# A softmax product skewed by two steps, and two engines given work ahead of the expert stages

## The chip, the cores and the metric

The kernel runs on one core of a Trainium2 chip. The core has five engines that run their own instruction streams and meet at semaphores: TensorE (matmuls, from weights that a separate instruction loads), VectorE, ScalarE (activation functions, from a table that has to be loaded for each family of functions), GpSimd (POOL) and SyncE (SP), which mostly issues DMAs. Matmuls write to PSUM, eight banks of 128 partitions by 512 float32. The metric is the device time of one execution in microseconds; lower is better.

## The reference

Six residual layers on x of shape (4, 1024, 128), each on a layer norm of x: a top-4-of-32 expert layer, a linear attention, the expert layer again, a top-2-of-8 expert layer with exact gelu ("L1_ffn"), a softmax attention ("L1_attn"), and the top-2 layer again. The change touches the last three and the two gates ahead of them. Cut to what matters:

```python
def _L1_attn_ref(x, P_q, P_k, P_v, P_o):           # x (4, 1024, 128), 16 heads of 64
    logits = einsum('bhmk,bhnk->bhmn', Q, K) * sqrt(64)
    logits = where(causal, logits, -inf)
    key_weights = softmax(logits, axis=-1)
    o = einsum('bhmm,bhmv->bhmv', key_weights, V)   # the diagonal of the weights only
    return einsum('bhmv,hdv->bmd', o, P_o)

def _L1_ffn_ref(x, Wg, W1, b1, W2, b2):             # 8 experts, 512 hidden, top 2
    gates = softmax(xt @ Wg)                        # idx1, idx2, w1, w2 from them
    xe[idx1, pos1] += xt; xe[idx2, pos2] += xt      # rows sorted by expert
    h = gelu(einsum('ecd,edf->ecf', xe, W1) + b1)
    ye = einsum('ecf,efd->ecd', h, W2) + b2
    return ye[idx1, pos1] * w1 + ye[idx2, pos2] * w2
```

So softmax needs of every query only the diagonal weight: exp(own score - max) over the sum of exp(score - max).

## The kernel before

**Order of stages.** `program()` builds eleven stages and each engine runs its part of them one after another: setup, the gated expert layer, keys and queries of the linear attention, `sorted_ffn` (the second gated layer, whose tail also routes and sorts rows for the top-2 experts), `moe_experts`, `moe_combine`, `softmax_diagonal`, `sorted_ffn` once more (values and output of the softmax attention, with the routing of the last layer), `moe_experts`, `moe_combine`. The order of work on each engine is written out by hand; there is no scheduler.

**Softmax** (`softmax_diagonal`, L2678 on). A unit is one pair of heads of one batch: 8 pairs times 4 batches, 32 units. Both heads of a pair lie in the 128 partitions, head 0 in rows 0 to 63 and head 1 in rows 64 to 127, so each score matmul uses 64 rows of TensorE. `ORDER = (1, 5, 6, 4, 2, 3, 7)` is the order of the query blocks q of 128 queries; block q has (q + 1) x 128 keys. Blocks 4 to 7 are done by `big` (L2841): for each head two halves of (q + 1) x 64 columns (320, 384, 448 and 512), each in its own bank, and each as three passes over high and low parts of the operands, so 6 matmuls a head, 12 a product. Blocks 0 to 3 are done by `little` (L2863). Each unit also projects the keys and queries of the unit after next (`project`, L2820, four groups of three matmuls of 512 columns, L2829 to L2831) and sums the diagonal scores (`diagonals`, L2855).

For each block and head VectorE adds the causal mask and takes the minimum (`lowest`, L2968), and ScalarE then does exp with the sum of the row (`exps`, L2949, at L2950), both in the score banks. VectorE works head 0, then head 1 of a block, and so does ScalarE. The eight banks go round as a ring (`first_bank`), and `wait_bank` makes TensorE wait until the last user of a bank is done: mostly the exponential of an earlier block (`exp_done`), for the first banks after the projections ScalarE's or VectorE's copy of a projection (`out_act`, `out_dve`). For example block 4 gets the banks of block 5, head by head, and block 7 those of block 4.

In `big` of before all four banks, of both heads, are waited for first, and then head 0 and head 1 take turns matmul by matmul:

```python
for a in range(2):
    for k in range(2):
        wait_bank(pe, (first_bank(u, n) + 2 * a + k) % BANKS, "exp_done", scored_before(u, n, a) + 1)
for p, (qs, ks) in enumerate(passes(u)):
    for k in range(2):
        for a in range(2):
            last = pe.matmul(...)
```

**Expert stages** (`moe_experts`). 23 blocks of 512 sorted rows. SP loads the rows of a block from HBM (`rows_from`) once all of them have been sent there: it waits for `sent`, the semaphores of the indirect DMAs that GpSimd issues in `send_rows` (L812 on). TensorE turns them (`turn`, L2274), ScalarE and VectorE make the high and low parts (L2354, L2406), TensorE makes four up-products of three matmuls (L2286 to L2288), ScalarE does gelu (L2332) and the rounded copy (L2340), VectorE the low part (L2378) and copies the expert's weights to where TensorE reads them (L2385, L2394), TensorE makes the down-products (L2298 to L2300). `iterations` starts with an iteration c = -1 that only turns block 0. TensorE enters after `sorted`, which VectorE sets at the end of `positions`. ScalarE's last work before is the exp of the gates (L1499).

## Time and profile before

| | us |
|---|---|
| runs | 1681.05, 1692.07, 1695.04 (median 1692.07) |
| profiled execution | 1686.52, span 1684.5 |
| TensorE matmul busy | 1409.7 (84%), 7981 instructions |
| VectorE busy | 1342.9 (80%) |
| ScalarE busy | 1034.0 (61%) |
| GpSimd busy | 859.0 (51%) |
| mean granted TensorE clock | 0.946 of full speed |

The first expert stage's head lies at about 654 us, its blocks run to about 815; softmax runs from about 874 to 1333; the second expert stage's head lies at about 1481 us. In the rows a line such as L2850 is a line of the kernel before, PE is TensorE's matmuls and PEld its weight loads, DVE is VectorE, ACT ScalarE. A row's last bracket is the idle time of the engine before it and what ended it. A group with x12 is twelve instructions in a row, and its duration runs from the first start to the last end. The granted clock is 1.00 at 2.4 GHz and 0.50 at 1.2 GHz.

### The profile page before, as it was taken

What the parts mean: (1) busy time and instruction counts of PE and PEld (TensorE: products, weight loads), DVE (VectorE), ACT (ScalarE), POOL (GpSimd) and SP (SyncE); (2) the same over time, 40 slices, a digit from 0 to 9 for tenths busy, and PEclk for the clock granted to TensorE, in tenths of its full rate; (3) what the DMA queues carried; (4) which work ended last, traced back from release to release, by engine and by line L of the source; (5) the groups of instructions that cost most, each with busy time, mean ns of one, the idle gap of its engine ahead of it and who ended that gap; (6) DMA issues with size and microseconds to landing.
All of it is one profiled execution on the core that took longest, in us unless ns stands there. A gap on an engine that the chain in (4) does not pass through costs nothing.

```text
span 1684.5 us, 29060 instructions
## 1 busy us (share of the span) xinstructions
PE 1409.7 (84%) x7981; PEld 1029.5 (61%) x7981; DVE 1342.9 (80%) x3812; ACT 1034.0 (61%) x2178; POOL 859.0 (51%) x743
## 2 busy tenths in 40 slices
PE   5999999898999994999358888888888799679990
PEld 4777877655656663777236665566566566457770
DVE  7699999567676766787679999999999777858876
ACT  7544442374232326888469999999989623268880
POOL 5856753210133342666656666666666225627662
PEclk9999999999999996999779999999999899879995
DMA  9990010000011104232299700000000001123225
GB/s 197 182 180 15 1 26 26 2 1 13 20 32 43 32 21 100 61 79 67 73 195 182 119 1 1 1 1 1 1 1 2 1 14 38 42 56 73 67 60 150
DMA packets 182167, 91.61 MB, mean 54 GB/s; under 512 B 43829, under 2 KB 176902, under 8 KB 182048
## 3 DMA queue, kind: packets, MB, share of 16 engines
q1 hardware_dynamic: 167840, 71.19, 23.2%
q0 software_dynamic: 9984, 16.89, 3.1%
q10 hardware_dynamic: 4224, 2.10, 0.4%
q8 instruction: 56, 0.92, 0.2%
q14 instruction: 63, 0.52, 0.1%
HBM read 32.59 MB, written 61.18 MB: 56 GB/s over the span
## 4 chain that ended last, share of the span: by engine, by line
PE 56%; DVE 16%; ACT 11%; issue 7%; DMA 3%; POOL 3%; DVEq 2%; SPq 1%; POOLq 0%; ACTq 0%
PE psum L1371 9%; PE psum L2850 8%; ACT psum L2950 7%; PE psum L660 5%; PE psum L661 4%; PE psum L662 4%; DVE psum L2970 4%; PE psum L2829 2%; PE psum L2830 2%; PE psum L2831 2%; DVEq L2418 2%; PE psum L1126 1%; DMA answers<-ed,answer_to 1%; PE psum L1128 1%; PE psum L1127 1%
## 5 line engine op out<-in xcount | busy, mean ns | idle before, releaser
L2970 DVE CUSTOM_DVE_ANT_0 psum<-psum,cmask 128x128 f32<-128x128 f32 (+7 forms) x512 | 375.1, 786 | 23.8 <-PE psum L2850 23.5
L2950 ACT ACTIVATE psum<-psum,gate 128x128 f32<-128x128 f32 (+7 forms) x512 | 367.0, 719 | 41.7 <-DVE gate L2970 34.4
L2462 POOL DMA_INDIRECT answers<-ed,answer_to x184 | 199.4, 1084 | 82.5 <-issue 47.4
L1371 PE MATMUL psum<-raw_all,w 128*128 128x512 f32 x384 | 196.6, 595 | 1.5 <-DVE raw_all L1512 1.5
L660 PE MATMUL psum<-xl,wreg 128*128 128x512 f32 x320 | 181.9, 568 | 2.6 <-ACT psum L2950 1.3
L1510 DVE SCALAR_TENSOR_TENSOR raw_all<-psum,hg 128x512 f32<-128x512 f32 x128 | 88.1, 690 | 58.5 <-PE psum L662 56.9
L2850 PE MATMUL psum<-spare_sets_room 64*128 64x384 f32 (+3 forms) x768 | 91.9, 371 | 43.1 <-ACT psum L2950 43.1
L2850 PE MATMUL psum<-hh,hl 64*128 64x384 f32 (+3 forms) x768 | 91.9, 371 | 41.9 <-ACT psum L2950 41.9
L661 PE MATMUL psum<-xh,wreg 128*128 128x512 f32 x320 | 126.9, 397 | 0.0
L662 PE MATMUL psum<-xh,wreg 128*128 128x512 f32 x320 | 126.7, 396 | 0.0
L2850 PEld LDWEIGHTS psum<-spare_sets_room 64*128 64x128 f32 x768 | 70.0, 190 | 67.4 <-ACT psum L2950 55.8
L2378 DVE TENSOR_TENSOR hl<-gate,hh 128x512 fp32r<-128x512 f32 x92 | 63.3, 688 | 59.7 <-ACT hh L2340 35.7
L2850 PEld LDWEIGHTS psum<-hh,hl 64*128 64x128 f32 x768 | 70.2, 191 | 66.4 <-ACT psum L2950 52.8
L1240 POOL TENSOR_TENSOR hl<-hg,hh 128x512 fp32r<-128x512 f32 x65 | 86.1, 1329 | 44.2 <-ACT hh L1172 37.3
L2950 ACT ACTIVATION_READ_ACCUMULATOR psum<-psum,gate 128x1 f32 x512 | 105.0, 205 | 0.0
L824 POOL DMA_INDIRECT rows<-raw_all,row_no x64 | 61.8, 965 | 74.5 <-PE psum L662 61.8
L824 POOL DMA_INDIRECT rows<-row,row_no x64 | 62.0, 969 | 64.8 <-PE psum L662 50.3
L1172 ACT ACTIVATE hh<-hg 128x512 fp32r<-128x512 f32 x86 | 54.1, 633 | 65.7 <-DVE hg L1203 63.8
L201 POOL TENSOR_TENSOR spare_p<-spare_p 128x1 f32<-128x1 f32 x63 | 18.3, 290 | 140.7 <-DVE row_no L785 66.6
L660 PEld LDWEIGHTS psum<-xl,wreg 128*128 128x128 f32 x320 | 61.3, 192 | 38.4 <-issue 26.5
L1371 PEld LDWEIGHTS psum<-raw_all,w 128*128 128x128 f32 x384 | 72.4, 189 | 20.2 <-DVE raw_all L1512 2.2
L661 PEld LDWEIGHTS psum<-xh,wreg 128*128 128x128 f32 x320 | 61.4, 192 | 32.6 <-issue 28.1
(437 smaller groups left out, 4051.3 us busy)
## 6 DMA issues: line engine op xcount, KB each, us to landing
rows<-blank SPq DMA_DIRECT2D x146, 258.0 KB, 7.2
row<-rows SPq DMA_DIRECT2D x46, 256.0 KB
raw_all<-answers SPq DMA_DIRECT2D x32, 256.0 KB, 4.2
w<-in_L_ffn_W_dram SPq DMA_DIRECT2D x16, 256.0 KB, 3.0
answers<-ed,answer_to POOLq DMA_INDIRECT x184
x<-in_L_attn_x_dram SPq DMA_DIRECT2D x4, 512.0 KB, 5.8
out_dram<-x ACTq DMA_DIRECT2D x8, 256.0 KB, 4.6
rawD<-in_L_ffn_values_dram SPq DMA_DIRECT2D x4, 256.0 KB, 6.9
```

The source lines that it names most:

```text
L660: pe.matmul(dst, wh, xl[:, blk(i)], start=start, stop=False)
L661: pe.matmul(dst, wl, xh[:, blk(i)], start=False, stop=False)
L662: return pe.matmul(dst, wh, xh[:, blk(i)], start=False, stop=stop)
L824: pool.indirect_dma_start(rows, bass.IndirectOffsetOnAxis(ap=row_no[:, i % 2, c, t:t + 1], axis=0), row_of(i)[:, t, c, :], None).then_inc( ...
L1240: pool.tensor_tensor(hl[:, j % SLOTS, :], kept[n % len(kept)], hh[:, j % SLOTS, :].bitcast(F32), ALU.subtract).then_inc(S["lo_pool"], 1)
L1371: pe.matmul(bank(B_OUT[i % 2]), col(dn, j), hidden[:, n % HID, :], start=(j == 0), stop=(j == nf - 1)).then_inc(S["dn_done"], 1)
L1510: last = dve.scalar_tensor_tensor(out, raw, 0.0, gates_now, ALU.max, ALU.mult)
L2378: dve.tensor_tensor(hl[:, j, :], hid[j], hh[:, j, :].bitcast(F32), ALU.subtract).then_inc(S["lo_done"], 1)
L2462: pool.indirect_dma_start(answers, bass.IndirectOffsetOnAxis(ap=answer_to[:, out.odd, t:t + 1], axis=0), y_row[:, out.odd, t, :], None, bo ...
L2850: last = pe.matmul(big_scores(u, n, a)[:, k, :], head(qs, a, q * P, P), head(ks, a, k * half, half), start=(p == 0), stop=(p == 2))
L2950: return act.activation(src, src, ACT.Exp, bias=kept_at(arg, u, q, a), scale=-1.0, accum_out=kept_at(esum, u, q, a))
L2970: return dve.tensor_tensor_reduce(src, src, mask, 1.0, 3e38, ALU.add, ALU.min, kept_at(arg, u, q, a))
```

## The change

Three edits. `big` issues head 0's six matmuls two steps ahead of head 1's (`SKEW = 2`): steps 0 and 1 of head 0 alone, then four steps of both in turn, then steps 4 and 5 of head 1 alone; and each bank is waited for just before its first matmul, not all four ahead. `keep_awake` runs matmuls of 512 bf16 columns whose result is not used, into bank 0: 7 at the entry of each expert stage, after waiting for `sent` of all rows, and 3 in the iteration c = -1, behind the turn of block 0. ScalarE runs one Gelu on a small tile (4 columns) after the exp of the gates, into `rs`, whose content is no longer needed; it waits for the last layer norm step first.

```diff
--- before.py
+++ after.py
@@ -824,6 +824,11 @@
                 pool.indirect_dma_start(rows, bass.IndirectOffsetOnAxis(ap=row_no[:, i % 2, c, t:t + 1], axis=0),
                                         row_of(i)[:, t, c, :], None).then_inc(S["sent"][i % 2], 16)
 
+    def keep_awake(pe, times):
+
+        for _ in range(times):
+            pe.matmul(bank(0), onesb[:], m16[:].rearrange("p e t -> p (e t)"), start=True, stop=True)
+
     def count_all(pe, S):
 
         pe.wait_ge(S["place_step"], PLACES * NB)
@@ -1497,6 +1502,8 @@
                 heads_turned(act, H)
             act.wait_ge(S["logits_scaled"], 1)
             act.activation(G, L, ACT.Exp).then_inc(S["exp_done"], 1)
+            act.wait_ge(S["step"], NORMS * NB)
+            act.activation(rs[:], mv[:, :, 1], ACT.Gelu)
 
         def vector(dve):
             def apply_gates(i, j):
@@ -2311,6 +2318,8 @@
                 for j in range(Q):
                     if j == 0 and (b + 1).there():
                         turn(b + 1)
+                    if j == 0 and not b.loop and b.c == -1:
+                        keep_awake(pe, 3)
                     if b.there():
                         up(b, j)
                     if (b + -1).there():
@@ -2319,6 +2328,9 @@
                         back(b + -2)
 
             pe.wait_ge(before["sorted"], 1)
+            for a in range(2):
+                pe.wait_ge(before["sent"][a], 16 * 2 * BT * (NB // 2))
+            keep_awake(pe, 7)
             iterations(pe, one)
 
         def scalar(act):
@@ -2699,6 +2711,7 @@
         ORDER = (1, 5, 6, 4, 2, 3, 7)
         LITTLE = {1: (1,), 2: (2, 0), 3: (3,)}
         DIAG, QUARTERS = 1, 4
+        SKEW = 2
         NS = 2 * len(ORDER)
         BANKS_OF = [4 if q >= BT else 2 for q in ORDER]
         PER_UNIT = NP + sum(BANKS_OF)
@@ -2841,16 +2854,23 @@
             def big(u, n):
                 q = ORDER[n]
                 half = wide(q) // 2
-                for a in range(2):
-                    for k in range(2):
+                steps = [(p, k) for p in range(3) for k in range(2)]
+
+                def step(a, m):
+                    p, k = steps[m]
+                    qs, ks = passes(u)[p]
+                    if p == 0:
                         wait_bank(pe, (first_bank(u, n) + 2 * a + k) % BANKS, "exp_done", scored_before(u, n, a) + 1)
-                for p, (qs, ks) in enumerate(passes(u)):
-                    for k in range(2):
-                        for a in range(2):
-                            last = pe.matmul(big_scores(u, n, a)[:, k, :], head(qs, a, q * P, P),
-                                             head(ks, a, k * half, half), start=(p == 0), stop=(p == 2))
-                            if p == 2 and k == 1:
-                                last.then_inc(S["scored"], 1)
+                    last = pe.matmul(big_scores(u, n, a)[:, k, :], head(qs, a, q * P, P),
+                                     head(ks, a, k * half, half), start=(p == 0), stop=(p == 2))
+                    if m == len(steps) - 1:
+                        last.then_inc(S["scored"], 1)
+
+                for m in range(len(steps) + SKEW):
+                    if m < len(steps):
+                        step(0, m)
+                    if m >= SKEW:
+                        step(1, m - SKEW)
 
             def diagonals(u):
                 g, b = which(u)
```

On TensorE, in softmax, from the diagonals (L2859, after: L2879) to the 320-column product, in a unit in the middle of a batch. The names in brackets are those of the first owner of a semaphore, which is used again here: `f0_oT_ready` is `exp_done`, `a0_kv_done` is `out_dve`, `a0_f_done` is `out_act`. Before:

```order
L2859 MATMUL psum<-ed,pair_ones 32x256 [waits f0_xT_done]
L2859 MATMUL psum<-ed,pair_ones 32x256 x3
L2850 MATMUL psum<-spare_sets_room 128x384 [waits a0_kv_done,f0_oT_ready]
L2850 MATMUL psum<-spare_sets_room 128x384 x11
L2850 MATMUL psum<-spare_sets_room 128x448 [waits f0_oT_ready,a0_f_done]
L2850 MATMUL psum<-spare_sets_room 128x448 x11
L2850 MATMUL psum<-spare_sets_room 128x320 [waits f0_oT_ready]
L2850 MATMUL psum<-spare_sets_room 128x320 x11
```

and of the change:

```order
L2879 MATMUL psum<-ed,pair_ones 32x256 [waits f0_xT_done]
L2879 MATMUL psum<-ed,pair_ones 32x256 x3
L2864 MATMUL psum<-spare_sets_room 128x384 [waits f0_oT_ready] x2
L2864 MATMUL psum<-spare_sets_room 128x384
L2864 MATMUL psum<-spare_sets_room 128x384 [waits a0_kv_done]
L2864 MATMUL psum<-spare_sets_room 128x384
L2864 MATMUL psum<-spare_sets_room 128x384 [waits a0_kv_done]
L2864 MATMUL psum<-spare_sets_room 128x384 x6
L2864 MATMUL psum<-spare_sets_room 128x448 [waits a0_f_done] x2
L2864 MATMUL psum<-spare_sets_room 128x448
L2864 MATMUL psum<-spare_sets_room 128x448 [waits f0_oT_ready]
L2864 MATMUL psum<-spare_sets_room 128x448
```

The row of the first matmul of a product carried all its waits; now four of its twelve matmuls carry one each: the first two of head 0, and the first of each half of head 1, with a matmul of head 0 between.

On TensorE, from the end of the gates (`count_all`, L831, after: L836) to the first up-product of the expert stage (L2286, after: L2293). Here `a0_f_ready`, `a0_scaled` stand for `x_load`, and `a0q_squared` for `xl_done`. Before:

```order
L831 MATMUL psum<-m,before 128x512 [waits f1_place_step,f1_g_copied,f1_hid_done]
L831 MATMUL psum<-m,onesb 128x512
L2274 MATMUL psum<-ident,row 128x128 [waits a0_f_ready,f1_sorted]
L2274 MATMUL psum<-ident,row 128x128 x3
L2274 MATMUL psum<-ident,row 128x128 [waits a0q_squared,a0_scaled]
L2274 MATMUL psum<-ident,row 128x128 x3
L2286 MATMUL psum<-xl,xh 128x512 [waits a0q_q_done,a0q_squared]
L2287 MATMUL psum<-xl,xh 128x512
```

and of the change:

```order
L836 MATMUL psum<-m,before 128x512 [waits f1_place_step,f1_g_copied,f1_hid_done]
L836 MATMUL psum<-m,onesb 128x512
L830 MATMUL psum<-m,onesb 128x512 [waits f1_sent1,f1_sent0,f1_sorted]
L830 MATMUL psum<-m,onesb 128x512 x6
L2281 MATMUL psum<-ident,row 128x128 [waits a0_f_ready]
L2281 MATMUL psum<-ident,row 128x128 x3
L830 MATMUL psum<-m,onesb 128x512 x3
L2281 MATMUL psum<-ident,row 128x128 [waits a0q_squared,a0_scaled]
L2281 MATMUL psum<-ident,row 128x128 x3
L2293 MATMUL psum<-xl,xh 128x512 [waits a0q_q_done,a0q_squared]
L2294 MATMUL psum<-xl,xh 128x512
```

Seven matmuls stand ahead of the first turn, with the waits for the row sends and for `sorted`, and three between the first and the second turn.

On ScalarE, from the exp of the gates (L1499, after: L1504) to the first gelu (L2332, after: L2344), before:

```order
L1499 ACT_TABLE_LOAD
L1499 ACTIVATE own<-own 128x256 [waits f1_logits_scaled]
L2354 ACTIVATE xl<-psum 128x512 [waits a0q_rooted,f1_sorted]
L2354 ACTIVATE xl<-psum 128x512 [waits a0q_rooted]
L2332 ACT_TABLE_LOAD [waits a0_ks_read]
L2332 ACTIVATE r<-psum,b_now 128x512 [waits a0q_den_done] x2
```

and of the change:

```order
L1504 ACT_TABLE_LOAD
L1504 ACTIVATE own<-own 128x256 [waits f1_logits_scaled]
L1506 ACT_TABLE_LOAD
L1506 ACTIVATE rs<-mv 128x4 [waits f1_step]
L2366 ACTIVATE xl<-psum 128x512 [waits a0q_rooted,f1_sorted]
L2366 ACTIVATE xl<-psum 128x512 [waits a0q_rooted]
L2344 ACTIVATE r<-psum,b_now 128x512 [waits a0_ks_read,a0q_den_done]
L2344 ACTIVATE r<-psum,b_now 128x512 [waits a0q_den_done]
```

The table load that stood behind the two rounded copies of rows, right ahead of the first gelu, now stands behind the exp. The instructions of VectorE, GpSimd and SP are the same in the same order.

## Rows read from the trace of the kernel before

**Rows 1.** Busy time by stretch: us, then busy (xinstructions) of each engine, granted clock, DMA

```profile
661.04:665.12 4.08, 4.08 (x12) 3.21 (x11) 1.44 (x4) 3.66 (x5) 0.00 (x0) 0.50 0.54 127
...
1488.21:1491.15 2.94, 2.94 (x9) 2.36 (x8) 1.44 (x4) 2.52 (x3) 0.00 (x0) 0.50 0.40 107
...
1021.49:1035.70 14.21, 11.59 (x95) 8.52 (x94) 13.45 (x36) 13.16 (x34) 9.14 (x6) 1.00 0.00 1
...
1166.88:1170.30 3.42, 3.42 (x28) 3.38 (x28) 2.50 (x7) 2.71 (x7) 3.42 (x2) 0.50 0.00 0
```

**Rows 2.** Timeline of one softmax unit: start us, us, engine, line, op [idle before, releaser]

```profile
1020.43 0.97 DVE L2970 CUSTOM_DVE_ANT_0 psum<-psum,cmask 128x768 f32<-128x768 f32 x1 [0.39 <-PE psum L2850]
...
1020.84 1.49 PE L2850 MATMUL psum<-hh,hl 64*128 64x448 f32 x12 [0.44 <-ACT psum L2950]
...
1021.31 1.00 DVE L2970 CUSTOM_DVE_ANT_0 psum<-psum,cmask 128x768 f32<-128x768 f32 x1
1021.49 0.88 ACT L2950 ACTIVATE psum<-psum,gate 128x768 f32<-128x768 f32 x1 [0.80 <-DVE gate L2970]
...
1022.33 1.10 DVE L2970 CUSTOM_DVE_ANT_0 psum<-psum,cmask 128x896 f32<-128x896 f32 x1
...
1023.65 1.14 PE L2850 MATMUL psum<-hh,hl 64*128 64x320 f32 x12 [1.33 <-ACT psum L2950]
...
1024.57 0.98 ACT L2950 ACTIVATE psum<-psum,gate 128x896 f32<-128x896 f32 x1
...
1024.80 0.83 DVE L2970 CUSTOM_DVE_ANT_0 psum<-psum,cmask 128x640 f32<-128x640 f32 x1 [0.27 <-PE psum L2850]
...
1025.73 0.77 ACT L2950 ACTIVATE psum<-psum,gate 128x640 f32<-128x640 f32 x1
...
1026.52 0.77 ACT L2950 ACTIVATE psum<-psum,gate 128x640 f32<-128x640 f32 x1
...
1027.65 1.65 PE L2850 MATMUL psum<-hh,hl 64*128 64x512 f32 x12 [0.86 <-ACT psum L2950]
...
1030.50 0.39 PE L2831 MATMUL psum<-xh,wreg 128*128 128x512 f32 x1
1030.50 0.19 PEld L2829 LDWEIGHTS psum<-xl,wreg 128*128 128x128 f32 x1
...
1030.72 0.39 PE L2829 MATMUL psum<-xl,wreg 128*128 128x512 f32 x1
...
1033.29 1.31 PE L2850 MATMUL psum<-spare_sets_room 64*128 64x384 f32 x12
...
1035.70 0.88 ACT L2950 ACTIVATE psum<-psum,gate 128x768 f32<-128x768 f32 x1 [0.81 <-DVE gate L2970]
```

**Rows 3.** Chain of waits in that unit: start us, us, what

```profile
1027.41 0.24 issue
```

**Rows 4.** Who waited for whom, 878 to 1320 us: total us, times, longest

```profile
DVE psum L2970 <- PE psum L2850: 21.9, 57, 1.2
```

**Rows 5.** Timeline of ScalarE, 1164 to 1180 us: q=5, head 0, of two units

```profile
1164.43 0.88 ACT L2950 ACTIVATE psum<-psum,gate 128x768 f32<-128x768 f32 x1 [0.81 <-DVE gate L2970]
...
1179.29 0.88 ACT L2950 ACTIVATE psum<-psum,gate 128x768 f32<-128x768 f32 x1 [0.83 <-DVE gate L2970]
```

**Rows 6.** Chain of waits of the whole span: the last row send

```profile
651.28 2.37 DMA rows<-row,row_no
```

**Rows 7.** Timeline of the first expert stage's head

```profile
657.65 1.09 PE L2274 MATMUL psum<-ident,row 128*128 128x128 f32 x4 [7.24 <-DMA row<-rows]
...
660.31 1.08 PE L2274 MATMUL psum<-ident,row 128*128 128x128 f32 x4 [1.56 <-DVE xl L2406]
...
662.04 1.28 ACT L2332 ACT_TABLE_LOAD   x1
...
663.34 1.34 ACT L2332 ACTIVATE r<-psum,b_now 128x512 f32<-128x512 f32 x2
...
666.89 0.40 PE L2298 MATMUL psum<-hh,xh 128*128 128x512 f32 x1
```

## The prediction

> **What bounds the kernel now.** I read the stretches by engine first, then who waited for whom in softmax, then one unit of softmax in order of time, last the head of an expert stage.
>
> Softmax is 32 units (8 pairs of heads, 4 batches), from about 878 to 1333 us. In a quiet unit no engine is full: VectorE 13.45, ScalarE 13.16, TensorE 11.59 of 14.21 us [rows 1]. What repeats is a loop through three engines, to be followed in [rows 2] (a "product" is a `big`, named by its columns per half; q is the row block). VectorE takes the minimum of q=5, head 0 (1020.43); ScalarE's exponentials of q=5, 6 and 4 follow almost without a gap (1021.49 to 1026.52 + 0.77, and the last is over, its sum read out, at 1027.41 [rows 3]); this frees the banks of the 512-column product (1027.65); behind it TensorE runs four projections, the small scores, the diagonals and the 384-column product (1033.29) without waiting; its head 0 starts VectorE 14.2 us after the first time. Exponentials start at 1021.49 and 1035.70: the period. VectorE waited for the products 21.9 us in 57 waits, 0.7 per unit [rows 4]. That 0.7 is the most that earlier scores can give back.
>
> The two expert stages start with a slow clock: granted 0.50, that is 1.2 of 2.4 GHz, while TensorE makes the first hidden products (661.04 to 665.12, and 1488.21 to 1491.15) [rows 1]. Before the first of them it had waited 7.24 us for the rows (657.65) [rows 7].
>
> **Softmax, part by part.** Nothing is added to the work: twelve matmuls as before, now in eight slots instead of six. A slot of 512 columns is 0.22 to 0.23 us (1030.50 to 1030.72) [rows 2]; scaled by columns, as an estimate, 0.17 for 384, 0.20 for 448, 0.14 for 320 (check: the twelve of 320 and of 512 columns take 1.14 and 1.65, 0.085 more a slot, the scale says 0.086).
> What the skew does to a product that waits: head 0 now asks only for its own banks, so its first steps run while head 1's exponential ends. After head 1's banks come free, head 0 needs three steps instead of six, head 1 still six. So head 0 is scored three slots earlier and TensorE is free at the same time as before. For one that doesn't wait, head 0 is as before and head 1 two slots later, the last of which the next product's head 0 can fill.
> - q=4, 320 columns (1023.65, waited 1.33): head 0 is there 0.42 earlier. VectorE had waited 0.27 (1024.80) and gets 0.27. ScalarE does not: its exponential before ends at 1024.57 + 0.98 = 1025.55 and the next could start at 1025.62 at the usual gap of up to 0.07, against 1025.73. Worth 0.11 to the loop.
> - q=6, 448 columns (1020.84 + 1.49 = 1022.33): VectorE starts exactly then, where an unhindered minimum starts 0.09 before its predecessor ends (1021.31 against 1020.43 + 0.97): it is 0.11 late. The product waited 0.44 for the small block's head 1; head 0 no longer does, less up to 0.34 for two solo slots of the 384-column product. Worth 0.10.
> - q=7, 512 columns (1027.65): TensorE is free when it was before, and all behind it in the loop hangs on that. Worth 0; head 0 early only makes slack for VectorE.
> - q=5, 384 columns (1033.29): no wait; head 0 needs six slots as before. Worth 0.
> Sum 0.21 a unit. Against it stand the waits: a product carries four instead of one or two, in mid-stream. A projection carries one too and still starts 0.22 after the matmul before it [rows 2]; that bounds it at 0 for wide matmuls. Above, an unmet wait shows 0.24 (1027.41 to 1027.65) [rows 3]; a met one should be well below, and three of them lie before head 0 of q=5 is done: up to 0.15 a unit. I take 0.04, since the projection is the nearest row. 0.17 x 31 periods = **5.3 us**; bounds 0.06 and 0.21, 1.9 and 6.5 us.
>
> **Clock inside softmax.** Four times in the stage the clock stood at 0.50 for 3.4 us, each time after a stretch in which TensorE waited for ScalarE; one is 1166.88 to 1170.30 [rows 1]. The unit it fell in took 14.86 instead of 14.21 (1164.43 to 1179.29) [rows 5]; at 0.65 the four cost 2.6. The skew moves work into just those waits. I take three of four away, **2.0 us**; bounds: four away (2.6), four more (-2.6).
>
> **Expert stages.** The last row send before the first stage lands at 651.28 + 2.37 = 653.65 [rows 6]. Then TensorE runs 7 wide bf16 matmuls, at half clock twice 0.22, so 3.1 us: to about 656.8, before the rows arrive for the first turn at 657.65 [rows 7]. They cost nothing, and if they overran, only the overrun. Their bank 0 is not used by anyone then. SP's loads don't wait for them. Three more go behind the first turn, in the 1.56 us wait before the second (660.31) [rows 7]. In the trace the clock came back after 4.1 and 2.9 us of unbroken work [rows 1], so by 658 it should be full, and the fillers leave idle stretches of about 1 us, no longer than softmax has at full clock (1.33) [rows 2].
> At full clock the second turn feeds the first up-product at 660.7 instead of 661.04. Twelve matmuls then save about 0.2 each until 665.1, together some 2.1. ScalarE now has Gelu's table already (its load moved behind the exponential, into idle time): the first Gelu waited 662.04 + 1.28 to 663.34 [rows 7] and can now start when the first product is there, 661.7. The first down-product (666.89) needs Gelu, rounding, the low part and VectorE's two weight copies: all 1.7 earlier; up-products 2.2 earlier. I take **1.9 us** a stage, **3.8** for both, the second alike; from there TensorE is full, so it stays. Bounds: 0.6 a stage if the clock doesn't hold and only the table counts, 2.3 if TensorE alone set it.
> VectorE, POOL and SP issue the same instructions in the same order.
>
> **Sum:** 5.3 + 2.0 + 3.8 = 11.1 us. The profiled execution took 1686.5 (span 1684.5), so 1675.4 by it. The runs shown lie at 1681.1 to 1695.0, median 1692.1; the four of them with the profiled one have a mean of 1688.7. I put the gain on a level between the two, 1690: **1679 us**, 0.8% under the median of before.
>
> **Rivals.**
> *The skew pays in full (0.12).* If TensorE's run from q=7 to q=5 starts earlier as well, the loop shrinks until VectorE is never late: 14.21 - 13.45 = 0.76 a unit [rows 1], 23.6 us. With 2.6 and 3.8: 30 us, 1660. For it: three slots on each of four products add up to 2.2 us. Against: the 512-column product's end does not move in my walk.
> *Waits eat the skew (0.16).* At 0.05 a wait, four waits a product, the loop stays at 14.2 and the clock falls as often. Left: 3.8 to 4.5, 1686.
> *The clock doesn't hold (0.06).* The idle second between fillers and first product drops it again; 0.6 a stage stays: 5.3 + 2.0 + 1.3 = 8.6, 1681.
> *Slower: a lone step can't hide its weight load (0.06).* In the solo slots the next weights go into the same 64 rows that are multiplying. If a load (0.19 [rows 2]) must wait there, q=5's head 0 has two such slots ahead and q=7's end two behind, all in the loop: 0.76 - 0.21 = 0.55 a unit, 17 us; less 3.8 it is 13 slower, 1703. It decides from 0.05 exposed per solo slot on. Against: the projections use all 128 rows, one after another, and the load of one starts with the matmul before it and is hidden (1030.50, both rows) [rows 2]. I leave it 0.06, since no 64-row matmul runs alone in this trace.
> The Trainium skill ("TensorE: Matmul & The Clock Gate", Part 3: Packing small matmuls) states that a weight load overlaps a running matmul only when their row groups differ. By that rule the slower rival would be the case; the row at 1030.50 does not agree with it.
>
> **Chances.** Forecast 0.60, rivals 0.12, 0.16, 0.06, 0.06. Measurement tells about 1% (17 us) here. Faster by more: the full rival and the upper end of my own case, 0.25. Slower by more: the far end of the slower rival, 0.04. Within: 0.71. Range: my bounds (6.3 to 12.9 gained, 3.6 if the clock falls more often) with 5 us for the level of the runs give 1672 to 1689; opening it towards the full rival, 1668 to 1690.
>
> **What would show it.** Period of a quiet unit 14.0 to 14.05; VectorE's wait before q=4, head 0, gone, the one before q=5 still 0.3 to 0.4; the 384-column head 0 no later relative to the diagonals (if it is 0.3 later, weight loads are exposed). At most two drops of the clock in softmax. At the expert stages granted clock 1.0 before the first up-product, Gelu without a load in front, first down-product 1.9 earlier. I am wrong if the period is below 13.8 or above 14.2.

## The result and the profile after

The changed kernel takes 1666.3 us (median of four runs, 1663.6 to 1667.3), before beside it 1687.8 (four runs): a ratio of 0.987, 95% interval 0.982 to 0.992. I had predicted 1679 and a range down to 1668; the gain is about twice what I gave it. The profiled execution's span went from 1684.5 to 1661.7, 22.8 us less.

The stretches by engine, one quiet unit of softmax and the heads of both expert stages (us; then busy time and instructions of each engine, granted clock, DMA), for [rows 1]:

```profile
1041.70:1055.47 13.77, 12.88 (x94) 9.55 (x92) 13.24 (x35) 12.85 (x35) 9.13 (x6) 1.00 0.00 1
...
659.52:663.60 4.08, 4.08 (x21) 3.29 (x19) 2.44 (x7) 3.52 (x7) 0.00 (x0) 0.95 0.55 127
...
1466.12:1470.20 4.08, 4.08 (x22) 3.10 (x19) 2.61 (x7) 3.70 (x7) 0.00 (x0) 1.00 0.55 126
```

The unit is 13.77 us long, not 14.21, and no engine is full yet. TensorE looks busier (12.88 instead of 11.59) with the same matmuls, because head 0's first steps now start early and run alone for a while. The up-products of both expert stages, 4.08 us, hold 21 and 22 matmuls at a granted clock of 0.95 and 1.00 instead of 12 at 0.50.

The timeline of that unit, for [rows 2]:

```profile
1041.70 0.97 DVE L2990 CUSTOM_DVE_ANT_0 psum<-psum,cmask 128x768 f32<-128x768 f32 x1 [0.40 <-PE psum L2864]
...
1042.76 0.88 ACT L2970 ACTIVATE psum<-psum,gate 128x768 f32<-128x768 f32 x1 [0.86 <-DVE gate L2990]
...
1043.80 0.70 PE L2864 MATMUL psum<-hh,hl 64*128 64x320 f32 x3 [0.56 <-ACT psum L2970]
...
1044.71 1.14 PE L2864 MATMUL psum<-hh,hl 64*128 64x320 f32 x9 [0.22 <-ACT psum L2970]
...
1045.59 0.86 DVE L2990 CUSTOM_DVE_ANT_0 psum<-psum,cmask 128x640 f32<-128x640 f32 x1
1045.62 0.19 ACT L2970 ACTIVATION_READ_ACCUMULATOR psum<-psum,gate 128x1 f32 x1
1045.77 0.98 ACT L2970 ACTIVATE psum<-psum,gate 128x896 f32<-128x896 f32 x1
...
1046.76 0.76 ACT L2970 ACTIVATE psum<-psum,gate 128x640 f32<-128x640 f32 x1
...
1047.78 2.35 PE L2864 MATMUL psum<-hh,hl 64*128 64x512 f32 x12
...
1048.21 0.21 ACT L2970 ACTIVATION_READ_ACCUMULATOR psum<-psum,gate 128x1 f32 x1
...
1048.47 1.23 PEld L2864 LDWEIGHTS psum<-hh,hl 64*128 64x128 f32 x9 [0.25 <-ACT psum L2970]
...
1056.53 0.88 ACT L2970 ACTIVATE psum<-psum,gate 128x768 f32<-128x768 f32 x1 [0.85 <-DVE gate L2990]
```

Head 0 of q=4 starts with three matmuls alone (1043.80) and the other nine follow at 1044.71; VectorE's minimum of q=4 (1045.59) and ScalarE's exponential (1046.76) now follow the work before them at once. The wait of 0.40 in front of q=5's minimum is as before. The surprise is in the chain of waits through the same unit, for [rows 3] (start us, us, what):

```profile
1042.76 1.92 ACT psum L2970 x4
1044.67 0.04 issue
1044.71 1.14 PE psum L2864 x9
```

Between ScalarE freeing a bank of the 320-column product and TensorE's matmul stand 0.04 us. In the same place of before's chain, and again in front of the 512-column product [rows 3], stood 0.24:

```profile
1023.41 0.24 issue
```

In the changed kernel the chain does not pass through ScalarE in front of the 512-column product, but the timeline above shows the same there: ScalarE has read out its last exponential of q=4 at 1048.21 + 0.21 = 1048.42, and head 1's first weight load starts at 1048.47.

Who waited for whom, 878 to 1300 us, for [rows 4]: VectorE on the scores fell from 21.2 us in 55 waits (the same stretch of before) to

```profile
DVE psum L2990 <- PE psum L2864: 9.9, 26, 0.5
```

The head of the first expert stage, for [rows 7], TensorE and then ScalarE:

```profile
652.27 3.15 PE L830 MATMUL psum<-m,onesb 128*128 128x512 bf16 x7 [3.54 <-DMA rows<-row,row_no]
656.11 1.11 PE L2281 MATMUL psum<-ident,row 128*128 128x128 f32 x4 [0.69 <-DMA row<-rows]
657.02 1.49 PE L830 MATMUL psum<-m,onesb 128*128 128x512 bf16 x3
658.78 1.09 PE L2281 MATMUL psum<-ident,row 128*128 128x128 f32 x4 [0.28 <-DVE xl L2418]
659.52 0.66 PE L2293 MATMUL psum<-xl,xh 128*128 128x512 f32 x1
...
664.02 0.50 PE L2305 MATMUL psum<-hh,xh 128*128 128x512 f32 x1 [0.20 <-DVE xh L2406]
```

```profile
650.25 1.28 ACT L1506 ACT_TABLE_LOAD   x1
...
660.68 1.37 ACT L2344 ACTIVATE r<-psum,b_now 128x512 f32<-128x512 f32 x2 [0.17 <-PE psum L2295]
```

The extra matmuls and the table load lie in idle time as planned. But in this stage the second turn still takes 1.09, the duration of half clock (0.63 in the second stage, at 1465.73), so the first up-product stands 3.41 us behind the first turn as before (3.39).

**Where 22.8 us went**, from one profiled execution of each kernel. From the first turn to the first down-product: 9.24 to 7.91 in stage 1 and 9.00 to 7.40 in stage 2, 1.33 + 1.60 = 2.9. Not all of it lasts: from the first turn to the last down-product stage 1 is 0.7 shorter and stage 2 0.9. From the exponential of q=5, head 0, in unit 0 to that in unit 31: 445.2 to 428.4, 16.8. Of these, 13.5 are 30 quiet periods by 0.45, 1.3 are two drops of the clock instead of four, and 1.9 the last period (13.75 to 11.86). In that last period before had a fifth drop, and e4 below, with before's waits and quiet period (but the skewed order) and no drop there, took 12.97: so I put the drop, as an estimate, at 0.8 of the 1.9. The rest of the 22.8, about 4.4, I cannot assign to the change: 1.5 had been gained by the first turn of stage 1 (1.4 of it when the last row send landed, ahead of the extra matmuls), and 3.0 lie between the last of those exponentials and the first turn of stage 2, where before spent 10.2 us at a granted clock of 0.50 from 1334.1 on and the changed kernel 3.4 us from 1315.3 on.

### The profile page after: what moved, and what is told of

It is laid out like the page before. It is cut to its first block, busy times and chain, and to the rows that moved or that the text cites. A ratio compares the mean times of both kernels' runs of the same rounds, so it can differ in the third digit from the quotient of the medians.

```text
span 1661.7 us, 28846 instructions
## 1 busy us (share of the span) xinstructions
PE 1448.9 (87%) x8001; PEld 1057.5 (64%) x8001; DVE 1337.1 (80%) x3812; ACT 1025.5 (62%) x2180; POOL 861.0 (52%) x743
## 4 chain that ended last, share of the span: by engine, by line
PE 61%; DVE 14%; ACT 8%; issue 7%; DMA 4%; POOL 3%; DVEq 2%; SPq 1%; POOLq 0%; ACTq 0%
PE psum L1376 9%; PE psum L2864 8%; PE psum L2889 5%; PE psum L660 5%; PE psum L661 4%; PE psum L662 4%; ACT psum L2970 4%; DVE psum L2990 3%; PE psum L2842 2%; PE psum L2843 2%; PE psum L2844 2%; PE psum L1131 1%; PE psum L1133 1%; DMA answers<-ed,answer_to 1%; PE psum L1132 1%
## 5 line engine op out<-in xcount | busy, mean ns | idle before, releaser
L2990 DVE CUSTOM_DVE_ANT_0 psum<-psum,cmask 128x128 f32<-128x128 f32 (+7 forms) x512 | 370.8, 790 | 12.6 <-PE psum L2864 11.3
L2864 PE MATMUL psum<-hh,hl 64*128 64x384 f32 (+3 forms) x768 | 113.4, 372 | 13.6 <-ACT psum L2970 13.6
L2864 PE MATMUL psum<-spare_sets_room 64*128 64x384 f32 (+3 forms) x768 | 114.1, 368 | 12.1 <-ACT psum L2970 12.1
L2864 PEld LDWEIGHTS psum<-hh,hl 64*128 64x128 f32 x768 | 86.5, 190 | 40.7 <-ACT psum L2970 33.8
L2970 ACT ACTIVATION_READ_ACCUMULATOR psum<-psum,gate 128x1 f32 x512 | 111.6, 218 | 0.0
L2864 PEld LDWEIGHTS psum<-spare_sets_room 64*128 64x128 f32 x768 | 85.4, 185 | 40.1 <-ACT psum L2970 34.2
```

What stands on the lines that cost most here:

```text
L2864: last = pe.matmul(big_scores(u, n, a)[:, k, :], head(qs, a, q * P, P), head(ks, a, k * half, half), start=(p == 0), stop=(p == 2))
L2970: return act.activation(src, src, ACT.Exp, bias=kept_at(arg, u, q, a), scale=-1.0, accum_out=kept_at(esum, u, q, a))
L2990: return dve.tensor_tensor_reduce(src, src, mask, 1.0, 3e38, ALU.add, ALU.min, kept_at(arg, u, q, a))
```

## Experiments

Periods are medians of the 31 distances between the exponentials of q=5, head 0, in neighbouring units. "Release" is the time from the end of the read-out of ScalarE's exponential of head 1 to the first matmul that it frees, ahead of the 320-column product (q=4) and of the 512-column product (q=7), as the median of the 32 units; the chain of waits counts it some 0.01 shorter. The gaps are the medians of the time between the end of the exponential before and ScalarE's first exponential of q=6 and of q=4 (the short read-outs between them are not counted). Drops are falls of the granted clock to 0.50 that begin between the exponentials of q=5, head 0, of unit 0 and of unit 31. All of these come from one profiled execution of each kernel. Ratios are against runs of before on the same chip; e7, e9, e10, e11 and e12 ran only once (1683.5, 1700.7, 1676.5, 1682.7 and 1679.9 us, against 1703.3 of before for the first two and 1699.1 for the others), so they have none.

| kernel | banks awaited | head 1 behind head 0 | release q=4, q=7 | gaps q=6, q=4 | period | drops | ratio (95%) |
|---|---|---|---|---|---|---|---|
| before | four ahead | 0 steps | 0.26, 0.25 | 0.23, 0.19 | 14.23 | 5 | 1 |
| changed | each at its step | 2 | 0.05, 0.05 | 0.17, 0.02 | 13.77 | 2 | 0.987 (0.982-0.992) |
| e1 | each at its step | 2 | 0.05, 0.05 | 0.17, 0.02 | 13.78 | 2 | 0.988 (0.986-0.990) |
| e2 | four ahead | 0 | 0.26, 0.26 | 0.22, 0.19 | 14.23 | 5 | 0.998 (0.996-1.000) |
| e3 | each at its step | 0 | 0.05, 0.05 | 0.17, 0.02 | 13.79 | 6 | 0.989 (0.987-0.992) |
| e4 | four ahead | 2 | 0.26, 0.25 | 0.23, 0.19 | 14.24 | 4 | 0.999 (0.997-1.001) |
| e6 | one ahead, merged | 0 | 0.05, 0.05 | 0.28, 0.02 | 13.91 | 4 | 0.994 (0.992-0.996) |
| e7 | each twice, at its step | 2 | 0.14, 0.14 | 0.17, 0.02 | 13.84 | 2 | |
| e8 | each at its step | 6 | 0.05, 0.05 | 0.17, 0.02 | 13.79 | 3 | 0.992 (0.989-0.994) |
| e9 | at its step for 512 columns, else ahead | 2 | 0.26, 0.05 | 0.32, 0.11 | 14.03 | 6 | |
| e13 | only those not yet met | 2 | 0.05, 0.05 | 0.17, 0.02 | 13.77 | 2 | 0.988 (0.987-0.990) |

### e1 and e2: the two halves of the change

e1 is the changed kernel without these lines and the waits in front of them, e2 has them and before's `big`:

```diff
-            act.activation(rs[:], mv[:, :, 1], ACT.Gelu)
...
-                        keep_awake(pe, 3)
...
-            keep_awake(pe, 7)
```

> The change's softmax part alone: head 1 two score steps behind head 0, each bank awaited at its own step; no extra matmuls and no early Gelu. Theory A (fewer waits in series behind the last exponential, and earlier head 0): quiet softmax period 13.77 as in the changed kernel (14.21 before), two to three stretches of half clock in softmax, expert stages as before (turn to first down-product 9.2 and 9.0 us); total 16 to 20 us faster than before. Rival B (the waking of the engines sets something in softmax, too): period above 13.9.

> The change's waking part alone: ten extra matmuls a stage and the early Gelu, scores as before. Theory A: period 14.21 as before, four or five stretches of half clock in softmax; turn to first down-product 7.9 and 7.4 us as in the changed kernel, so 1.3 and 1.6 us from the two stages; total 3 us faster, up to 5 with the end of softmax. Rival B (the extra matmuls bring softmax a different clock history): fewer than four drops, more than 5 us faster.

e1: 1687.7 against 1706.8 us of before, period as in the changed kernel. e2: 1704.8, 0.2% (2 us) faster with an interval that touches no change; its quiet period is 14.23, and from the first turn to the first down-product it takes 7.41 and 6.94 us, less than the 7.9 and 7.4 I had expected from the changed kernel. The score part carries nearly everything, the waking has no effect on the quiet period of softmax. Rival B falls in both: e1's period is below 13.9, and e2's clock fell as often as before's.

### e3 and e4: the order of the steps, and the place of the waits

e3 is e1 with the two heads in turn again, but every bank still awaited at the step that first writes it:

```diff
-        SKEW = 2
+        SKEW = 0
```

e4 is e1 with the waits back in front:

```diff
+                for a in range(2):
+                    for k in range(2):
+                        wait_bank(pe, (first_bank(u, n) + 2 * a + k) % BANKS, "exp_done", ...)
                 def step(a, m):
...
-                    if p == 0:
-                        wait_bank(pe, (first_bank(u, n) + 2 * a + k) % BANKS, "exp_done", ...)
```

> Scores of the two heads in turn as before, but each bank awaited at the step that writes it first instead of four waits in front of the product. Head 0 gets one slot of head start, not three. Theory A (waits in series behind the release cost 0.17 us per loop, the earlier head 0 the rest): the 512-column product starts 0.1 or less after the exponential instead of 0.24, period 13.85 to 13.98, about 8 us faster. Rival B (the order of steps is what pays, waits cost nothing): lag stays at 0.24, period 14.1 to 14.2. Rival C (met waits in mid-stream cost): slower than 14.2.

> Head 1 two steps behind head 0 as in the change, but all four banks awaited in front of the product as before. Theory A (what pays are the release with one wait and head 0 starting before head 1's banks are free): neither is there, so the lag is 0.24 and the period 14.15 to 14.3, total as before within 5 us. Rival B (the staggered order pays by itself, since head 0 is done earlier relative to head 1): 14.0 or less. Rival D (solo slots expose weight loads): above 14.4.

This is the pair that decides. The order alone (e4) gives nothing: 14.24. The place of the waits alone (e3) gives the whole period, 13.79. Theory A holds, and was still too cautious for e3: I had expected a period of 13.85 to 13.98 and about 8 us, and 16 us came (1690.9 against 1706.8): one slot of head start fills ScalarE's gaps as well as three. The chain of waits of e3 at the 512-column product has the short release without any skew:

```profile
1060.34 3.71 ACT psum L2963 x8
1064.05 0.04 issue
1064.10 1.66 PE psum L2857 x8
```

### e6 and e7: how many waits stand in series

e6 is before, with the four waits of a product merged into one per semaphore, with the highest count; the steps keep their old order:

```diff
+        def wait_banks(pe, some):
+            due = {}
+            for k, freed, count in some:
+                if k in last_user:
+                    s, c = last_user[k]
+                    due[id(s)] = (s, max(c, due[id(s)][1]) if id(s) in due else c)
+                last_user[k] = (S[freed], count)
+            for s, c in due.values():
+                pe.wait_ge(s, c)
```

e7 is e1 with each wait written twice:

```diff
                         wait_bank(pe, at, "exp_done", scored_before(u, n, a) + 1)
+                        if due:
+                            pe.wait_ge(*due)
```

> The kernel before, its scores in their old order, but the four waits in front of a product merged into one per semaphore with the highest count. Theory A1 (waits in series behind the release cost it all, as every product that waits starts 0.2 us earlier): exponential to product 0.17 instead of 0.37 us, gap before q=4's exponential 0.02 instead of 0.19, period 13.77 to 13.85. Theory A2 (q=4 and q=6 need head 0 ahead of head 1's banks): only the lag falls, period 14.0 to 14.05. Rival B (the number of waits costs nothing, only their place): 14.2.

> The staggered order with each bank's wait given twice in a row; the second is always met. Theory A: one more wait behind the release costs some 0.1 us where TensorE stands still: lag 0.25 to 0.3 instead of 0.17, period 13.85 to 13.95. Rival B (met waits are free): 13.77, lag 0.17. Rival C (met waits hold up the products that don't wait, too): above 14.0.

e6 falls between its two theories: 13.91. All of head 1's banks are still asked for before head 0 starts, and yet 0.32 of the 0.45 are there: 0.20 from the release and 0.12 from the gaps (0.42 to 0.30 together; q=4's is filled as in the changed kernel, q=6's is not). So what a late wait adds beyond fewer waits is q=6's gap, 0.28 to 0.17, another 0.11. Rival B, that the number of waits costs nothing, is refuted. In e7 one met wait more behind the one that releases costs 0.10 in the chain, at the same place as 1044.67 above:

```profile
1054.62 0.14 issue
1054.75 1.12 PE psum L2861 x9
```

and 0.06 a period (13.84). That is less than theory A had (13.85 to 13.95), but not nothing, as rival B had it, and rival C, that met waits hold up all products, is refuted.

The traces show what the time goes into. Between the release and the weight load that opens the product, TensorE's queue runs two separate semaphore instructions in before, e2, e4 and, at q=4, e9 (in before at 1027.44 and 1027.54, one with a single wait and one with two; the fourth wait rides on the weight load), one in e7, and none where the product waits for its banks one at a time or merged. This holds in all 32 units, and the weight load follows 0.22, 0.11 and 0.05 us after the end of the read-out.

### e8: head by head

e8 is e1 with head 1 a whole product of steps behind:

```diff
-        SKEW = 2
+        SKEW = 6
```

> Each bank awaited at its step, and head 1 six steps behind head 0, so written head by head. Theory A (the two halves of the rows take their work apart from each other, so that the order between heads costs nothing): period 13.77 to 13.85 as with two steps or none. Rival B (TensorE keeps the order written): the 384- and 512-column products take up to six slots more each, period above 15. Between them, 13.9 to 14.6, if head 1 can overtake some steps but not six.

The period is 13.79: the order between the heads costs nothing even when one is written wholly before the other. For the 384-column product in the unit at 1067 us, the stretch of 1.25 us that ends with head 0's scores, that line's instructions alone (us; PE busy, PEld busy, clock):

```profile
1067.55:1068.80 1.25, 1.25 (x12) 1.25 (x14) 1.00 0.05 13
```

Twelve matmuls lie in the time of seven slots of 0.17 to 0.18: eleven of this product and the first of the next one's head 0. Head 1's first, written behind all six of head 0, starts at 1067.94, 0.46 after head 0's first, and the first matmul of the next product (1068.63) starts ahead of the last two of this product's head 1 (1068.75 and 1068.92). So the two heads' matmuls run beside each other and out of the order in which they are written. Rival B is refuted.

### e9: one product alone

e9 is e1 with late waits for the 512-column product only:

```diff
+                for a in range(2 * (q < 7)):
+                    for k in range(2):
+                        wait_bank(...)
...
-                    if p == 0:
+                    if p == 0 and q == 7:
```

> Head 1 two steps behind head 0, but only the 512-column product awaits each bank at its own step; the other three await all four banks ahead, as before. Theory A (two separate places: the 512-column product's release in the loop, 0.20; and the head start of q=4 and q=6 on ScalarE, 0.24): lag before the 512-column product 0.17, gaps before the exponentials of q=4 and q=6 unchanged (0.19, 0.23), period 14.0 to 14.05. Rival B (one place does it all): 13.8, or 14.2.

14.03, as theory A had it: 0.20 of the 0.45 come from the release of the 512-column product alone. One detail was wrong: the two gaps did not stay at 0.23 and 0.19 but moved to 0.32 and 0.11, with the same sum. At q=4 the four waits ahead and the long release are still to be seen, in its chain of waits:

```profile
1059.94 1.92 ACT psum L2966 x4
1061.86 0.25 issue
1062.10 1.15 PE psum L2860 x12
```

### e10, e11 and e12: the heads of the expert stages

e10 is the changed kernel without the early Gelu, e11 without the ten extra matmuls, e12 with more of them. The edit of e12:

```diff
-                        keep_awake(pe, 3)
+                        keep_awake(pe, 6)
-            keep_awake(pe, 7)
+            keep_awake(pe, 9)
```

> The changed kernel without the early Gelu: the ten extra matmuls a stage stay. First turn to first down-product was 9.24 and 9.00 us before (stages 1 and 2), 7.91 and 7.40 after the change. Theory A (both parts are needed, since either the table load or the slow clock alone keeps the first down-product late): the load of 1.28 us stands in front of Gelu again and 8.7 to 9.1 us are seen in both stages. Rival B (the clock alone sets it): 7.9 and 7.4 stay.

> The changed kernel without the ten extra matmuls a stage: the early Gelu stays. Theory A: the clock is half until 4 us after the first up-product as before, Gelu starts without a load, first turn to first down-product 8.3 to 8.6 us in both stages, so about half of the gain of 1.3 and 1.6. Rival B (the table alone sets it): 7.9 and 7.4. Rival C (the first down-product hangs on TensorE's half clock alone): 9.0 to 9.2 as before.

> The changed kernel with 9 and 6 extra matmuls a stage instead of 7 and 3. Theory A (in stage 1 the granted clock was still half at the second turn, because the unbroken work began too late): clock full before the first up-product in both stages, turn to first up-product 3.1 us and to first down-product 7.4 or less in both. Rival B (more matmuls only delay the rows' turn): first up-product 0.2 to 0.6 us later after the first turn, first down-product no earlier than 7.9 and 7.4.

From the first turn of each stage, us to the first up-product, the first Gelu and the first down-product:

| kernel | stage 1 | stage 2 |
|---|---|---|
| before | 3.39, 5.69, 9.24 | 3.39, 5.69, 9.00 |
| e1 (neither) | 3.39, 5.68, 9.00 | 3.39, 5.69, 9.20 |
| e11 (Gelu) | 3.39, 5.05, 8.99 | 3.39, 5.06, 9.66 |
| e10 (matmuls) | 2.91, 5.10, 8.33 | 3.07, 5.26, 8.49 |
| changed | 3.41, 4.58, 7.91 | 3.07, 4.05, 7.40 |
| e13 (both) | 2.61, 3.58, 6.94 | 3.07, 4.05, 7.40 |
| e2 (both) | 3.08, 4.06, 7.41 | 2.60, 3.59, 6.94 |
| e12 (more) | 2.55, 3.53, 6.88 | 3.01, 3.99, 7.34 |

The table load alone gives nothing (8.99 and 9.66, so rival C for e11; without either edit the sixteen stages of before, e1, e3, e4 and e6 to e9 took 8.93 to 9.24), the matmuls alone 0.5 to 0.9: 8.3 and 8.5, less than the 8.7 to 9.1 that I had expected of e10. With the clock up, the load is what stands in front of Gelu, in e10:

```profile
660.33 0.60 ACT L2364 ACTIVATE xl<-psum 128x512 fp32r<-128x512 f32 x1 [1.54 <-PE psum L2279]
660.95 1.28 ACT L2342 ACT_TABLE_LOAD   x1
662.24 1.27 ACT L2342 ACTIVATE r<-psum,b_now 128x512 f32<-128x512 f32 x2
```

Only both together give 1.3 to 2.4. Where the clock was full earliest, 2.06 (e2, stage 2), 2.30 (e13, stage 1) and 2.36 (e12, stage 1) came, about my upper bound of 2.3. e12 in stage 1 shows it, four turns in 0.60 instead of 1.09:

```profile
656.94 3.79 PE L830 MATMUL psum<-m,onesb 128*128 128x512 bf16 x9 [3.72 <-DMA rows<-row,row_no]
660.57 0.60 PE L2281 MATMUL psum<-ident,row 128*128 128x128 f32 x4
661.01 1.46 PE L830 MATMUL psum<-m,onesb 128*128 128x512 bf16 x6
662.74 0.63 PE L2281 MATMUL psum<-ident,row 128*128 128x128 f32 x4 [0.27 <-DVE xl L2418]
```

The additional fillers did not delay the second turn, which refutes rival B. But e12's stage 2 (7.34) is like the changed kernel's, and with 7 and 3 matmuls e2 had 6.94 there and e13 6.94 in stage 1: which it is differs between profiles with the same extra matmuls, and whether more of them make the early case more frequent is not settled by one profile.

### e13: only the waits that are needed

e13 is the changed kernel with

```diff
+                old, due = last_user[k]
+                if awaited.get(old, 0) < due:
+                    pe.wait_ge(S[old], due)
+                    awaited[old] = due
```

and in `little` head 1's bank awaited at head 1's first step.

> The changed kernel with each wait on a count that TensorE has already awaited left out, and the small blocks, too, awaiting head 1's bank only at head 1's first step. Theory A (in the changed kernel what is left in front of the product are waits that ride on weight loads and cost nothing; only the small block's second wait can still give a little): period 13.70 to 13.78, total within 3 us of the changed kernel, that is 20 to 24 us faster than before. Rival B (each wait left has a cost of some hundredths): period below 13.7.

Period 13.77, 1677.5 us against 1699.1 of before on that chip, ratio 0.988, as the changed kernel. In its chain of waits the issue of 0.11 ahead of the small block has shrunk,

```profile
1046.49 1.14 PE psum L2867 x9
1047.63 0.01 issue
1047.65 2.01 PE psum L2892 x15
```

but the small block does not set the period. The met waits left out here, which stood behind a step already running, had cost nothing measurable. No kernel tried here beats the changed one by more than the noise.

## Why the prediction was wrong

**The step that failed** is the one on the 512-column product: "TensorE is free when it was before, and all behind it in the loop hangs on that. Worth 0", with its companion "Against it stand the waits ... I take 0.04". Both went wrong in the same place. I read the 0.24 between exponential and product [rows 3] as the fixed price of a wait that isn't met, and asked what more waits would add. It was the price of four waits in series in front of one product, for which two semaphore instructions still ran after the release: with a single wait in front of head 1's step 0.04 remain. TensorE was thus free 0.20 earlier, not when it was before. e9 isolates it (14.23 to 14.03), e6 shows the same release with the old order of steps, and e7 puts a wait back and finds 0.10 in the chain. The sign of my waits term was wrong: 31 x (0.20 + 0.04) = 7.4 us, most of the 8.7 that are missing in softmax.

**The gaps on ScalarE** were right in mechanism and nearly in size: I had 0.11 + 0.10 = 0.21 a unit for q=4 and q=6, measured 0.17 + 0.06 = 0.23. But I ascribed them to the skew by two steps. e3 without skew has them too, and e4 with skew but early waits has not. What does it is that head 0's wait no longer includes head 1's banks, and at q=4 the earlier release suffices (e6).

**The other two products**: q=5's wait of 0.40 on VectorE stayed, as forecast. The period of 13.77 lies below the 13.8 that I had named as the mark of a wrong prediction.

**The clock in softmax**: I had 2.0 us for three drops of four; it is 1.3 for two of four, and about 0.8 more from a fifth, in the last unit of before, that I had missed. That the sum, 2.1, is so near is luck. Two drops in e1, e7 and e13, three in e8 and e10 to e12, against four to six in before, e2, e3, e4, e6 and e9: in these counts late waits alone (e3: six) don't do it, skewed order alone (e4: four) doesn't either, both together seem to. It would be the one thing that the skew brings, but it isn't shown: each count is of one execution, and although the medians of e1 and e3 differ by 3.2 us on the same chip (four drops by about 0.65 are 2.6), e3's fastest run, 1685.1, lies below all of e1's.

**The expert stages**: 1.9 each forecast, 1.33 and 1.60 measured. The mis-sized step is "by 658 it should be full": in stage 1 the granted clock was 0.50 until 659.9,

```profile
656.40:659.90 3.50, 3.22 (x12) 1.99 (x11) 1.70 (x2) 0.60 (x1) 0.00 (x0) 0.50 0.26 65
```

so the second turn was slow; in stage 2 it rose at 1465.4, just ahead of the second turn. That "from there TensorE is full, so it stays" did not hold in full either: by the last down-product 1.6 of the 2.9 were left in these two profiles. On the chip of e1 to e4 the length of a stage (first turn to last down-product) was 165.2 to 169.0 us without the extra matmuls (e1, e3, e4) and 164.6 and 164.8 with them (e2), so how much of the gain lasts is not settled. Also my bound of 0.6 for the table alone was too high: e11 finds none, though its first Gelu came 0.6 earlier; the first down-product then hangs, as far as e10 and e11 tell, on up-products at half clock.

**The rivals.** "The skew pays in full" had the right premise, that TensorE's run from q=7 to q=5 starts earlier, and the wrong end: the loop shrinks by 0.45, not 0.76, and VectorE still waits 0.40 in front of q=5. "Waits eat the skew" is refuted, with the opposite sign. "The clock doesn't hold" is refuted: it rose late but did not fall again over the up-products (0.95 and 1.00). The slower rival is refuted: in the changed kernel's solo slots, three matmuls of head 0 with 512 columns (that line's instructions alone)

```profile
1047.77:1048.46 0.69, 0.68 (x3) 0.40 (x3) 1.00 0.00 0
```

start 0.25 and 0.23 apart, and head 1 joins 0.22 after the third, the pace of paired ones, with a weight load for the same 64 rows in each slot. The load of the second (1047.80 to 1047.99) lies within the first matmul (1047.78 to 1048.19). The rule of the Trainium skill named in the prediction ("TensorE: Matmul & The Clock Gate", Part 3) is not what this row shows.

**Sum**, by the same terms: softmax 5.3 forecast, 14.0 measured (31 by 0.45); clock 2.0 and about 2.1; expert stages 3.8 and 2.9 at the first down-product, 1.6 at the last; and 0.7 more in the last period, for which I had no term. That is 11.1 against some 18.4, with about 4.4 us outside that I cannot assign to the change. My range was also narrower than my own bounds: all of them together give 1.9 - 2.6 + 1.2 = 0.5 to 6.5 + 2.6 + 4.6 = 13.7, not 6.3 (or 3.6) to 12.9. Even 13.7 falls short of what was measured, so it is the term of 0 for the 512-column product and not the adding up that made the forecast wrong.

## What to carry to other kernels

A short idle time between a releaser and the released engine is not one number: count the semaphore waits in front of the instruction, and merge those that a later or higher one implies, or put each at the step that needs it. A wait placed ahead of a group asks for the last resource before the first piece of work starts, so look first at where the waits stand and only then at the order of the work. When several things are changed at once, try order and waits apart: here the order was the visible edit and the waits were nearly the whole gain.

## What the runs showed of the hardware

- Of several waits in front of one matmul, some become semaphore instructions of their own, and each of these that still runs after the release adds about 0.10 us: from the end of the read-out to the first matmul 0.05 us with none (changed kernel, e3, e6), 0.14 with one (e7) and 0.25 to 0.26 with two (before, e2, e4), in the median of 32 units. Waits at steps behind a running matmul cost nothing measurable (e13 against the changed kernel, 13.77 both).
- Matmuls on the two halves of TensorE's rows are not bound to the order in which they are written: with six steps of head 0 written first, 12 ran in 1.25 us where one half alone makes seven, and head 1's first started 0.46 us after head 0's first (e8).
- The same kernel's level differs by about 1% between sessions, on different chips (before: 1687.8, 1706.8, 1703.3 and 1699.1 us). It doesn't lie in softmax, whose quiet period in e1 and in the changed kernel is the same to 0.01 us in two sessions, but for the greater part in the expert stages: from the first turn to the last down-product e1 took 167.5 and 168.3 us, before in the first session 158.0 and 159.1 and the changed kernel 157.3 and 158.2. What is slower there these runs don't settle.
